# A chunk's normalized tokens are turned by a DMA transpose of two 16-bit planes, not by TensorE

## What is computed

```python
xn = layernorm(x)
# attention, within each sequence
w = exp(tanh(((xn @ W + b) @ xn.T) * lw))        # lw: 1 / distance of two tokens, 0 on the diagonal
w = w * off_diag
att = (w / (w.sum(-1) + EPS)) @ xn
# mixture of experts, 8 experts with 176 hidden units, each token uses 2
scores = sigmoid(xn @ gate_w.T)
gates = scores where (scores + expert_bias) is among the token's two largest, else 0
h = square(relu(gates[e] * (xn @ w_up[e].T)))     # bf16 products
routed = sum over e of h @ w_down[e].T
shared = square(relu(xn @ shared_w_up.T)) @ shared_w_down.T
out = x + att + routed + shared
```

## Time and profile before

| what | value |
|---|---|
| three runs, median | 117.22 us (117.0 to 117.27) |
| the profiled execution, its own time | 117.67 us |
| its span in the trace | 115.9 us |
| instructions | 2796 |
| ACT, busy | 89.6 us (77%) |
| HBM read, written | 3.84 MB, 2.10 MB |

### The profile page before, as it was taken

The page is one execution under the profiler, slowest core; times in us unless marked ns, Lnnn a source line. Parts: engine busy times, 40 slices in busy tenths (PEclk is TensorE's granted clock), DMA queues, the critical chain, the costliest instruction groups (busy, mean ns, idle before and its releaser), DMA issues.

```text
span 115.9 us, 2796 instructions
## 1 busy us (share of the span) xinstructions
PE 109.8 (95%) x899; PEld 85.1 (73%) x914; DVE 100.8 (87%) x319; ACT 89.6 (77%) x139; POOL 62.0 (53%) x126
## 2 busy tenths in 40 slices
PE   3998999999999999999999999999999999999991
PEld 3965558787868776869588776879588767859790
DVE  6969989999898989989998989888998689989751
ACT  4454899987689987969799687969699687897760
POOL 6438853599968485635943585636942520613200
PEclk9999999999999999999999999999999999999999
DMA  2999305886775759593849939593949648696982
GB/s 100 306 246 304 123 0 113 73 170 125 138 142 113 188 100 190 56 228 64 169 80 221 124 72 177 105 162 78 172 86 218 118 90 165 118 217 129 138 207 91
DMA packets 47965, 16.56 MB, mean 143 GB/s; under 512 B 45008, under 2 KB 45904, under 8 KB 47952
## 3 DMA queue, kind: packets, MB, share of 16 engines
q1 hardware_dynamic: 47376, 15.44, 66.1%
q0 software_dynamic: 288, 0.72, 3.5%
q10 hardware_dynamic: 288, 0.23, 0.6%
HBM read 3.84 MB, written 2.10 MB: 51 GB/s over the span
## 4 chain that ended last, share of the span: by engine, by line
PE 93%; issue 2%; DVE 1%; POOL 1%; ACT 0%; DVEq 0%; POOLq 0%
PE out_ps L1033 16%; PE h_ps L984 14%; PE side L961 12%; PE dots L940 11%; PE out_ps L1021 6%; PE out_ps L1015 4%; PE small L925 4%; PE side L974 4%; PE small L897 4%; PE out_ps L1063 4%; PE small L881 3%; PE h_ps L997 2%; PE small L906 1%; PE side L916 1%; PE side L925 1%
## 5 line engine op out<-in xcount | busy, mean ns | idle before, releaser
L702 DVE SCALAR_TENSOR_TENSOR gated<-h_ps,gates 128x1408 bf16<-128x1408 f32 x28 | 45.3, 1617 | 4.6 <-PE h_ps L984 4.2
L509 ACT ACTIVATE hidden<-gated 128x1408 bf16<-128x1408 bf16 x30 | 41.1, 1380 | 2.6 <-DVE gated L702 1.6
L1033 PE MATMUL out_ps<-downT,hiddenT 128*128 128x128 bf16 x341 | 22.8, 219 | 0.0
L1033 PEld LDWEIGHTS out_ps<-downT,hiddenT 128*128 128x128 bf16 x341 | 20.8, 98 | 2.4 <-issue 0.6
L984 PE MATMUL h_ps<-upT,xnTb 128*128 128x512 bf16 (+1 forms) x71 | 18.5, 359 | 0.8 <-issue 0.2
L961 PEld LDWEIGHTS side<-xn,probs 128*128 128x128 f32 x120 | 15.1, 191 | 1.5 <-issue 0.5
L961 PE MATMUL side<-xn,probs 128*128 128x129 f32 x120 | 15.8, 274 | 0.0
L940 PE MATMUL dots<-projT,xnT 128*128 128x256 f32 x60 | 15.4, 379 | 0.0
L313 POOL TENSOR_SCALAR_AFFINE_SELECT probs<-probs 128x256 f32<-128x256 f32 x16 | 6.6, 410 | 15.2 <-ACT probs L466 15.1
L984 PEld LDWEIGHTS h_ps<-upT,xnTb 128*128 128x128 bf16 x84 | 7.1, 98 | 9.5 <-issue 3.2
L940 PEld LDWEIGHTS dots<-projT,xnT 128*128 128x128 f32 x60 | 10.8, 190 | 3.9 <-issue 1.7
(11 more groups left out here) (118 smaller groups left out, 181.4 us busy)
## 6 DMA issues: line engine op xcount, KB each, us to landing
x_sb<-in_x SPq DMA_DIRECT2D x7, 256.0 KB, 8.4
out_y<-final SPq DMA_DIRECT2D x7, 256.0 KB, 2.5
hiddenT<-hidden SPq DMA_TRANSPOSE x31, 3.6
upT<-in_up POOLq DMA_DIRECT2D x1, 352.0 KB, 6.7
downT<-in_down POOLq DMA_DIRECT2D x1, 352.0 KB, 8.0
late_sb<-in_late SPq DMA_DIRECT2D x1, 192.0 KB, 6.1
x_sb<-in_x SPq DMA_DIRECT2D x1, 128.0 KB, 2.5
x_sb<-in_x ACTq DMA_DIRECT2D x1, 128.0 KB, 2.7
```

The costliest lines, as they stand in the source:

```text
L509: a.activation(hidden[:, t, :], gated[:, t, :], ACT.Square).then_inc(squared, 1)
L702: v.scalar_tensor_tensor(out=gated[:, t, :].rearrange("p (e h) -> p e h", e=E), in0=h_ps[:, 0:NH].rearrange("p (e h) -> p e h", e=E), scal ...
L1033: last = t_.matmul(out_at(c, t), hiddenT[:, c % 2, t, j, :], downT[:, j, :], start=(t == 0 and j == 0 and c < LAST), stop=((t >= 2 or c == ...
```

## The change

From chunk BY_DMA = 3 on, PE no longer turns xn. POOL's `split` copies the chunk's xn, read as 16-bit words, into two planes of 128x512, low and high halves. SP issues one DMA transpose of 128x1024 words (`turn_planes`, 8 blocks). ACT's `merge` copies the turned planes as 16-bit integers into the two halves of each 32-bit word of `xnT`. `narrow` and `rest` wait for the merge instead of for `take_xT`. In POOL's loop `rsqrt` and `normalize` of the next chunk move ahead of `add_x` and `square_rest`, with `split` behind them.

```diff
+        planes = sb("planes", [P, 2, 2, TILES, D], U16)
+        planesT = sb("planesT", [P, 2, 2, CH], U16)
...
+            def turn_planes(c):
+                sp.wait_ge(planes_split, merges(c))
+                wait(sp, xT_merged, merges(c - 2))
+                sp.dma_start_transpose(
+                    planesT[:, c % 2, :, :].rearrange("p h (t n) -> p (h t) n", n=P),
+                    planes[:, c % 2, :, :, :].rearrange("p h t d -> p (h t d)")
+                ).then_inc(planes_turned[c % 2], 16)
...
             for k in range(1, NCH):
                 turn(k - 1, 0)
                 turn(k - 1, 1)
+                if k == 2:
+                    turn_planes(3)
+                elif 2 < k < NCH - 1:
+                    turn_planes(k + 1)
                 turn(k - 1, 2)
...
+            def split(c):
+                pool.wait_ge(xn_ready, xns(c, TILES - 1))
+                wait(pool, planes_turned[c % 2], planes_count(c) - 16)
+                g.tensor_copy(planes[:, c % 2, :, :, :],
+                              xn[:, c, :, 0:D].bitcast(U16).rearrange("p t (d h) -> p h t d", h=2)
+                              ).then_inc(planes_split, 1)
...
             normalize(3)
             narrow(2)
+            split(3)
             square_rest(1)
...
             for k in range(3, NCH + 1):
                 f, c = k, k - 1
+                if k + 1 < NCH:
+                    rsqrt(k + 1)
+                    normalize(k + 1)
+                    split(k + 1)
                 add_x(c)
                 if f < NCH:
                     square_rest(f)
-                if k + 1 < NCH:
-                    rsqrt(k + 1)
-                if k + 1 < NCH:
-                    normalize(k + 1)
...
+            def merge(c):
+                act.wait_ge(planes_turned[c % 2], planes_count(c))
+                wait(act, sup_made, c - 3)
+                wait(act, dots_made, Q * (c - 3))
+                wait(act, xTb_ready, c - 3)
+                a.activation(xnT[:, c % 4, :].bitcast(U16).rearrange("p (n h) -> p h n", h=2),
+                             planesT[:, c % 2, :, :], ACT.Copy).then_inc(xT_merged, 1)
...
             relu_shared(1)
-            take_xT(3)
             take_tanh(2, 1)
             square(1, 3)
             take_exp(2, 1)
+            merge(3)
...
                 take_tanh(f, 0)
-                if f + 1 < NCH:
-                    take_xT(f + 1)
                 take_exp(f, 0)
                 square(c, 3)
+                if f + 1 < NCH:
+                    merge(f + 1)
                 take_tanh(f, 1)
                 take_exp(f, 1)
...
-                elif c > 2:
-                    pe.wait_ge(proj_taken, c)
...
+                if c >= BY_DMA:
+                    pe.wait_ge(proj_taken, c)
+                    pe.wait_ge(xT_merged, merges(c))
                 for h in range(2):
-                    if c > 0 or h == 1:
+                    if 0 < c < BY_DMA or c == 0 and h == 1:
                         pe.wait_ge(xT_taken, c + 1)
...
             up_tile(1, 3)
-            transpose_x(3)
             dots(2, 1)
...
                 up_tile(c, 3)
-                if f + 1 < NCH:
-                    transpose_x(f + 1)
                 dots(f, 1)
```

More of the change, by code:

```diff
@@ L9 @@
 BF16 = mybir.dt.bfloat16
+U16 = mybir.dt.uint16
 I32 = mybir.dt.int32
@@ L123, in moe_attention_kernel @@
         xT_made, xT_taken, xTb_ready = sem("xT_made"), sem("xT_taken"), sem("xTb_ready")
+        planes_split, planes_turned, xT_merged = (
+            sem("planes_split"), [sem(f"planes_turned{par}") for par in range(2)], sem("xT_merged"))
         top_found, pair_set, marks_set, hot_step = sem("top_found"), sem("pair_set"), sem("marks_set"), sem("hot_step")
@@ L150, in moe_attention_kernel @@
         K = 2
+        BY_DMA = 3
         MARK = 2.0 ** 127
@@ L199, in hT_count, with merges, planes_count @@
             return 16 * (c // 2 + 1)
+        def merges(c):
+            return c - BY_DMA + 1
+        def planes_count(c):
+            return 16 * ((c - BY_DMA) // 2 + 1)
         block = ctx.enter_context(nc.Block())
@@ L301, in finish_decay @@
                                     channel_multiplier=1).then_inc(decay_made, 1)
+            def split(c):
[4 more added lines that the diff above has]
+                              ).then_inc(planes_split, 1)
             def narrow(c):
-                pool.wait_ge(xT_taken, c + 1)
+                if c < BY_DMA:
+                    pool.wait_ge(xT_taken, c + 1)
+                else:
+                    pool.wait_ge(xT_merged, merges(c))
                 if c == 0:
```

## The result

| | before | after |
|---|---|---|
| median | 117.25 us (4 runs, 117.0 to 117.62) | 119.62 us (4 runs, 119.19 to 120.21) |
| ratio, 95% interval | | 1.0204 [1.0171, 1.0237] |
| profiled execution, its span | 117.67, 115.9 us | 119.51, 117.8 us |

The change costs 2.4 us where 0.2 were forecast. The first page lines answer to the earlier trace rows: PE's busy time went down by 1.4 us and the span up by 1.9, so PE waits now.

The account below looks back on a forecast made before the run. The prediction took TensorE, busy 109.8 of 115.9 us, to bound the kernel. It summed -2.19 (transposes) + 2.04 (chunk 3 wait) + 0.2 (restart) + 0.1 (ties) = +0.15 us, forecasting 117.4 us, range 116.8 to 118.9.

Parts of the forecast that it names:

- Five groups of four transposes, 2.19 us off PE: PE, chunks 3 to 7: the transposes of xn leave its stream, 5 x 0.44 = 2.19 us less.
- Split 1.04 us, landing 3.6 us: GpSimd's copy of 1024 elements takes 1.04 us; the planes' DMA transpose lands 3.6 us after issue.
- M = 1.06 us: ScalarE: M, merge's duration for 1024 16-bit elements, priced by element count; bounds 0.61 and 1.38 us.
- rival 1: Merge dearer than its element count, deciding from M = 1.12 on; at 1.38, +1.4 us, 118.6 us; chance 0.20.
- the formula: Whole change with M open: -2.19 + (0.98 + M) + 0.2 + 4 x (M - 1.12, where positive).
- It waits 2.04 us: Chunk 3: PE reaches the weights of rest(3) at 37.76, merge(3) is seen at 39.80, so PE waits 2.04 us.
- A margin of 0.06 us: Loop, four periods: merge seen by PE at 63.61, PE at the weights of rest at 63.67; 0.1 us in all.
- the restart: PE at chunk 3: a stopped PE costs a little more to restart, 0.2 us.
- has no idle time from which to make this up: PE after the chunk 3 wait: no idle time to recover the 2.04 us; DVE only waits longer.
- Rival 3: Planes come late in their ring: 13.6 us long, 1.1 us on each of up to four periods, 119 to 122 us; chance 0.12.
- nearly all of the gain is handed back: The sum: of the 2.19 us taken off PE, nearly all returns in one wait at chunk 3; +0.15 us remains.
- a ring that turns in every period: Loop: merge, exp, mask, narrow, normalize, split, transfer, merge; 11.5 us long against a period of 12.51.

Follow-up runs that it names:

- e4: Changed kernel, merge writing its 16-bit elements next to each other (high plane taken twice, so xnT is not right): 118.59 us, 1.0103 of the kernel before.
- e1: Changed kernel with merge(3) moved from behind take_exp(2, 1) to ahead of take_tanh(2, 1): 118.8 us, 1.0118 of the kernel before.
- e7: Changed kernel with PE's down_tile(0, 1) moved from behind attend(1, 0) to behind up_tile(1, 1): 120.6 us, 1.0191 of the kernel before.
- e13: e7 with eight identity matmuls ahead of rest(3), filling PE's wait for ScalarE: 119.13 us.
- e2: e1 with the loop's merge(f + 1) also moved ahead of square(c, 3): 119.96 us, 1.0225 of the kernel before.
- e8: Changed kernel with the moves of e1 and e7, and merge writing densely while reading the planes by turns: 117.74 us, 1.0015 of the kernel before.

## Why the prediction was wrong, point by point

- *Five groups of four transposes, 2.19 us off PE*: right. With nothing late (e4, later periods) the period is 12.52 us, forecast 12.51.
- *Split 1.04 us, landing 3.6 us*: 1.04 and 3.5, right.
- *"M = 1.06 us"*: **this is the step that failed**, 1.34. It was read from rows that all write next to each other; e4 (1.04) shows that the count was rightly priced and the pattern not priced at all. It was rival 1, whose formula gives -2.19 + 2.32 + 0.2 + 0.88 = +1.2 us for 1.34; I gave it 0.20.
- *"It waits 2.04 us"* at `rest(3)`: the mechanism is right to the instruction. e1 takes the wait away and 2.13 us go from that stretch. That the numbers agree too (merge from 38.76, forecast 38.69; PE's idle time 2.07) is luck: with M = 1.34 the formula gives 2.32, and the trace of after comes to `rest(2)` 0.82 us earlier than before (21.43 for 22.25) and then loses 0.91 at the late hidden tile, which pushed PE and ScalarE's chain by different amounts.
- *"A margin of 0.06 us", in four periods*: gone with M. By the formula a period should be 12.73; it is 12.83. 0.06 of the difference is the hand-over from merge to PE, for which I had allowed 0.05 us and which takes 0.11 (65.74 to 65.85); that is the whole margin. So PE is held from about M = 1.06 on and not from 1.12, and the measured periods rise with merge from there: 12.52 at 1.04, 12.64 at 1.16, 12.83 at 1.34. The other 0.04 stays open; it may be the restart that I had charged to chunk 3 alone, and no run here prices that. Together 0.4 us in four periods.
- *What the sum did not have at all*: the late hidden tile of chunk 0 (0.91 us of wait in the trace, about 0.4 us by the executions of e7 and e13 at full clock), 0.6 us behind `rest(7)`, of which the tile at 110.31 makes 0.4 (0.1 to 1.5 in the variants), and the granted clock, which a PE idle for 2 us put at risk (1.5 us between the medians of e7 and e13, but little in the median of the changed kernel: its three executions at full clock have 119.51, all four 119.62). The forecast said that PE "has no idle time from which to make this up" and did not ask what an idle PE does to its clock.
- *Rival 3, planes late*: wrong for the change as it is, right for every version that asks for them earlier (e1 at chunk 4, e2 everywhere, e8).
- *-2.19 + 2.04, "nearly all of the gain is handed back"*: more than all was handed back, and 0.3 us of one duration, at chunk 3 and in four periods, is the largest part of what was missing. Measured: 1.2 us by the formula, 0.4 by periods longer than the formula has them; the remaining 0.8 of the 2.4 are argued and not shown: the late tiles (about 0.4 for the one of chunk 0, 0.4 in one trace for the last one) and the clock, in shares that these runs do not settle.

## What to carry to other kernels

A copy that moves from behind one producer to another has a new place in its engine's order; where an unrolled part meets a loop, work that place out on its own, since the steady state says nothing about it. Price a strided write by a row with that stride, or by both bounds, when the result stands at the head of a ring that turns in every period: 0.3 us of it were paid five times here. And a wait of 2 us on TensorE can cost more than its length, since its clock may fall behind it, as it did in 7 of 15 executions here. Moving an instruction up on one engine also moves what stands behind it down: in e1 that was the exp for which GpSimd, and so the next transfer, waited.

## What the runs showed of the hardware that I had not expected

- ScalarE, 1024 elements of 16 bits: 1.04 us written densely, 1.34 written to every second place (integers and bfloat16 alike), 1.16 written densely and read by turns from two places 1 KB apart.
- A granted clock of 1.2 GHz for some 3 us after PE had been idle for 1.79 us, beginning about a microsecond after it had gone back to work; seen so in one trace. A mean clock below 0.99 is in 7 of 15 executions of the kernels with that wait, in none of six with the wait filled by matmuls, and in two others.
- DMA transposes of the same 352 KB tile land after 3.5 us mostly, and after 4.0 to 5.3 us at single places of each execution, in the kernel before as well. Which tiles are hit differs between kernels with the same code up to there.
